# Eight transfers of the experts' weights in place of one, and no product of the mixture at place 2 of a chunk, in a two-layer GRU with a mixture of experts

## What is computed

```python
# part 1: two GRU layers over 1024 steps, batch 2, 256 features
mixed = tanh(x @ W_in.T + b_in + ctx)
h1 = gru(mixed, Wih0, Whh0, bih0, bhh0)    # r, z = sigmoid; n = tanh(xn + r * hn)
h2 = gru(h1, Wih1, Whh1, bih1, bhh1)       # h = (1 - z) * n + z * h, one step after the other
x = x + (gate[:, None, :] * h2 + h2) @ W_out.T + b_out
# part 2: one shared expert and 2 of 8 routed ones for each of the 2048 tokens
shared = silu(x @ w1) * (x @ w3) @ w2
s = sigmoid(concat(x, t_emb) @ router_W); top 2 of s + router_bias -> combine (N, 8)
routed = sum_e combine[:, e] * (gelu(x @ W1e[e]) @ W2e[e])
x = x + (shared + routed) / 3
```

## Time and profile before

| | us |
|---|---|
| median of 3 runs | 2195.91 (2191.42 to 2199.89) |
| the profiled execution | 2187.54 |
| its span | 2185.8 |
| TensorE busy in the span | 2068.4 |
| VectorE busy | 1841.5 |
| last state of layer 0 written (L424) | at 2116 |
| last state of layer 1 written | at 2156 |
| last group's work after that | to 2185.8 |
| instruction queue of TensorE (q8) | 548 packets, 8.98 MB |

### The profile page before, as it was taken

How to read it: one execution, slowest core, us unless ns; L and a number is a source line. 1 busy time by engine, 2 the same in 40 slices (tenths; PEclk the granted TensorE clock), 3 DMA queues, 4 the chain that set the end, 5 groups by cost and what they waited for, 6 DMA issues and landing times.

```text
span 2185.8 us, 162058 instructions
## 1 busy us (share of the span) xinstructions
PE 2068.4 (95%) x69920; PEld 1485.0 (68%) x69920; DVE 1841.5 (84%) x11225; ACT 1201.4 (55%) x6471; POOL 560.5 (26%) x2542
## 2 busy tenths in 40 slices
PE   6989899999999999999999999999999999999987
PEld 3666666677666776767767676666767676777766
DVE  4888889888888888888888888888888888888874
ACT  2555555555555555555555555555555555555542
POOL 1222232222322223222222222222232222222220
PEclk9999999999999999999999999999999999999999
DMA  5000000000000000000000000000000000000000
GB/s 219 4 4 5 4 5 5 24 5 5 9 5 24 5 5 10 5 24 5 10 5 24 5 5 9 5 24 5 5 10 5 24 5 10 5 21 9 5 16 19
DMA packets 10879, 32.76 MB, mean 15 GB/s; under 512 B 1368, under 2 KB 6832, under 8 KB 9136
## 3 DMA queue, kind: packets, MB, share of 16 engines
q1 hardware_dynamic: 10160, 22.38, 2.8%
HBM read 20.22 MB, written 2.16 MB: 10 GB/s over the span
## 4 chain that ended last, share of the span: by engine, by line
PE 60%; DVE 26%; ACT 10%; issue 3%; DMA 1%; SPq 0%; POOL 0%; DVEq 0%; POOLq 0%
PE bank L333 29%; PE bank L325 17%; PE bank L272 11%; DVE n_first L404 9%; DVE cells L424 7%; ACT factors L472 6%; ACT cells L476 4%; DVE r_pre L395 4%; DVE z_pre L405 3%; PE bank L306 3%; DVE bank L413 1%; DVE n_second L380 0%; DVE x L687 0%; PE bank L657 0%; DVE hid L745 0%
## 5 line engine op out<-in xcount | busy, mean ns | idle before, releaser
L333 PE MATMUL bank<-w_h,cells 128*22 128x128 f32 (+4 forms) x32768 | 1363.4, 281 | 23.6 <-DVE cells L424 13.9
L333 PEld LDWEIGHTS bank<-w_h,cells 128*22 128x22 f32 (+4 forms) x32768 | 853.0, 111 | 130.5 <-DVE cells L424 91.3
L325 PEld LDWEIGHTS bank<-w_h,cells 128*2 128x2 f32 (+15 forms) x28112 | 512.2, 113 | 528.1 <-DVE cells L424 502.8
L517 POOL TENSOR_SCALAR cells<-cells 128x4 f32<-128x4 f32 x2048 | 463.6, 226 | 1525.8 <-DVE cells L424 1524.8
L325 PE MATMUL bank<-w_h,cells 128*2 128x64 f32 (+15 forms) x28112 | 770.1, 225 | 76.3 <-DVE cells L424 55.5
L466 ACT ACTIVATE n_second<-r_pre 128x4 f32<-128x4 f32 x2048 | 426.3, 208 | 508.8 <-DVE r_pre L395 466.3
L472 ACT ACTIVATE factors<-z_pre 128x4 f32<-128x4 f32 x2048 | 429.6, 210 | 436.5 <-DVE z_pre L405 358.8
L404 DVE STREAM_TRANSPOSE n_first<-bank 128x64 f32<-128x64 f32 x2048 | 600.0, 293 | 33.1 <-PE bank L333 23.7
L424 DVE TENSOR_TENSOR_SCAN cells<-factors,cells 128x18 f32<-128x18 f32 x2048 | 397.2, 194 | 241.5 <-ACT cells L476 177.1
L395 DVE STREAM_TRANSPOSE r_pre<-bank 128x64 f32<-128x64 f32 x2048 | 480.6, 235 | 33.3 <-PE bank L325 24.9
L405 DVE STREAM_TRANSPOSE z_pre<-bank 128x64 f32<-128x64 f32 x2048 | 427.4, 209 | 0.0
(11 more groups left out here) (91 smaller groups left out, 558.8 us busy)
## 6 DMA issues: line engine op xcount, KB each, us to landing
c_all<-weights SPq DMA_DIRECT2D x6, 1024.0 KB
x_t<-in_x_t SPq DMA_DIRECT2D x4, 512.0 KB, 7.4
w_1e<-in_w_1e SPq DMA_DIRECT2D x1, 2048.0 KB
w_2e<-in_w_2e SPq DMA_DIRECT2D x1, 2048.0 KB
w_x<-in_w_x SPq DMA_DIRECT2D x2, 768.0 KB, 8.2
w_h<-in_w_h SPq DMA_DIRECT2D x2, 768.0 KB, 9.5
w<-in_w SPq DMA_DIRECT2D x3, 512.0 KB
out_y<-y SPq DMA_DIRECT2D x6, 256.0 KB, 3.5
```

What stands on the lines that cost most here:

```text
L325: mm = pe.matmul(r_sums[l][p][32 * g:32 * g + B * (j + 1)], state_tile(l, j, kt), w_h[l][:, kt, g, 2 * U:], start=False, stop=False, tile_ ...
L333: mm = pe.matmul(sums[l][p][32 * g:32 * g + B * (j + 1), 0:width], state_tile(l, j, kt), w_h[l][:, kt, g, 0:width], start=False, stop=Fals ...
L517: pool.tensor_scalar(cell_part(step_rows(l, j), 3), cell_part(step_rows(l, j), 1), 0.5, None, ALU.mult)\
```

## The change

The broadcast of a group's weights is cut into eight transfers, one for each expert, each issued when the one before has landed (by a wait of SP on a semaphore of their own, which is never cleared). Expert e's `hid` waits for its own transfer. The planner lets `hid` of expert 0 stand 8 half slots after `comb_t` and counts 2 more for each next expert, where it counted 12 for all; in the last group it counts 12 for all, as before. And in the groups of 128 steps (sparse windows) no product stands at place 2 of a chunk.

```diff
-    def transfer(self, name, after, took):
-        self.when[name], self.engine[name], self.value[name] = self.when[after] + took, "spread", 32
-        self.signals[name] = after
+    def transfer(self, name, after, took, value):
+        self.when[name], self.engine[name], self.value[name] = self.when[after] + took, "spread", value
...
         if engine == "pe":
-            return j in projection_pieces(part ^ 1) or part == 1 and (self.sparse or self.window > 5 * CH and j % 8 != 6)
+            return j in projection_pieces(part ^ 1) or self.sparse and j == 2 or part == 1 and (self.sparse or self.window > 5 * CH and j % 8 != 6)
...
-                    sp.dma_start(weights[:, 0:n], comb_t[0:E, 0:n]).then_inc(spread, 16)
-                if m == mix.when["comb_t"] // 2 + 1:
-                    sp.wait_ge(spread, 16)
-                    sp.dma_start(c_all[:, :, 0:n], weights[:, 0:n].partition_broadcast(P)).then_inc(spread, 16)
+                    sp.dma_start(weights[:, 0:n], comb_t[0:E, 0:n]).then_inc(s_spread, 16)
+                for e in range(E):
+                    if m == mix.when["comb_t"] // 2 + 1 + (e if mix is not mixtures[-1] else 0):
+                        sp.wait_ge(s_spread, mix.value[f"spread{e}"] - 16)
+                        sp.dma_start(c_all[:, e, 0:n], weights[e, 0:n].partition_broadcast(P)).then_inc(s_spread, 16)
...
-                            mix.add("dve", f"hid{u}_{m}{q}", (f"act{u}_{m if LAST else KT - 1}", f"down{u - 2}") + (("spread",) if i == m == q == 0 else ()),
+                            mix.add("dve", f"hid{u}_{m}{q}", (f"act{u}_{m if LAST else KT - 1}", f"down{u - 2}") + ((f"spread{i}",) if m == q == 0 else ()),
...
-            mix.transfer("spread", "comb_t", 12)
+            spread_before = 16 * (1 + E) * mixtures.index(mix)
+            for e in range(E):
+                mix.transfer(f"spread{e}", "comb_t", 8 + 2 * e if mix is not mixtures[-1] else 12, spread_before + 16 * (e + 2))
```

More of the change, by code:

```diff
@@ L70, in __init__ @@
         self.ops = {k: [] for k in ("pe", "act", "dve")}
-        self.when, self.value, self.engine, self.signals = {}, {}, {}, {}
-    def transfer(self, name, after, took):
-        self.when[name], self.engine[name], self.value[name] = self.when[after] + took, "spread", 32
-        self.signals[name] = after
+        self.when, self.value, self.engine = {}, {}, {}
+    def transfer(self, name, after, took, value):
+        self.when[name], self.engine[name], self.value[name] = self.when[after] + took, "spread", value
     def add(self, engine, name, waits, issue, beside=False, even=False):
@@ L100, in half @@
     def half(self, name):
-        return self.when[self.signals.get(name, name)] // self.window
+        return self.when[name] // self.window
     def total(self, engine, half):
@@ L108, in past_half @@
         mine = [o for o in self.ops[engine] if o[0] // self.window == half]
-        late = [k for k, o in enumerate(mine) if any(self.half(w) != half for w in o[2])]
+        late = [k for k, o in enumerate(mine) if any(self.half(w) != half for w in o[2] if self.engine[w] != "spread")]
         if late or half == 0:
@@ L218, in gru_moe_kernel @@
         s_hist = sem("s_hist")
+        s_spread = sem("s_spread")
         KINDS = ("r", "pe", "turn", "for_n", "n", "for_h", "h", "pool", "bias", "x", "xn", "go")
         sets = [[{k: sem(f"s_{k}{l}_{p}") for k in KINDS} for p in range(2)] for l in range(2)]
-        m_sets = [{k: sem(f"m_{k}_{p}") for k in ("pe", "dve", "act", "spread", "out", "go")} for p in range(2)]
+        m_sets = [{k: sem(f"m_{k}_{p}") for k in ("pe", "dve", "act", "out", "go")} for p in range(2)]
         def numbers(semaphores):
@@ L604, in sp_slots @@
                     sp.sem_inc(m_sets[half]["go"], 1)
-                spread = m_sets[mix.half("spread")]["spread"]
                 if m == mix.when["comb_t"] // 2:
                     wait_for(sp, mix, "comb_t")
-                    sp.dma_start(weights[:, 0:n], comb_t[0:E, 0:n]).then_inc(spread, 16)
-                if m == mix.when["comb_t"] // 2 + 1:
-                    sp.wait_ge(spread, 16)
-                    sp.dma_start(c_all[:, :, 0:n], weights[:, 0:n].partition_broadcast(P)).then_inc(spread, 16)
+                    sp.dma_start(weights[:, 0:n], comb_t[0:E, 0:n]).then_inc(s_spread, 16)
[3 more added lines that the diff above has]
+                        sp.dma_start(c_all[:, e, 0:n], weights[e, 0:n].partition_broadcast(P)).then_inc(s_spread, 16)
                 if m == mix.when[mix.y_done] // 2:
@@ L629, in wait_for @@
         def wait_for(eng, mix, name):
-            eng.wait_ge(m_sets[mix.half(name)][mix.engine[name]], mix.value[name])
+            if mix.engine[name] == "spread":
+                eng.wait_ge(s_spread, mix.value[name])
+            else:
+                eng.wait_ge(m_sets[mix.half(name)][mix.engine[name]], mix.value[name])
         def mixture_at(eng, engine, s, part, base):
```

## The result

The change makes the kernel slower by 0.4%: 2208.06 us against 2200.09, medians of 16 runs each on one chip, ratio 1.0037 (95% interval 1.0025 to 1.005). The forecast was 2185.0 with a range to 2194; it has the wrong sign. The profiled execution took 2205.99 us, its span is 2204.2.

What follows compares the result with a forecast made beforehand. The steps' scans set the pace (1.000 us each, 1.027 with mixture), with TensorE stalling for its own instructions behind broadcasts. Terms -12.0 + 0.8 - 2 - 0.3 + 2.6 = -10.9 us took 2195.91 to 2185.0; range 2176 to 2194.

Steps and rivals of the forecast that it cites:

- (f): Last group, which nothing hides: eight chained 64 KB pieces at 1.7 us each make the end 2.6 us later.
- rival 1: Last group's pieces cost 2.2 us each, so the tail grows by 6.6 us and the time is 2189.0; chance 0.17.
- (a): Steps: cutting the broadcast removes TensorE's stalls on its instruction blocks behind it, 12.0 us gained.
- (b): Steps: the pieces delay some of the 28 instruction blocks that pass by them, 0.8 us lost in all.
- rival 2: Steps: pieces hold instruction blocks up nearly as the whole did; from 0.43 us per block (a)'s gain is gone; chance 0.12.
- (c): Steps: SP's chained transfers come early enough that VectorE doesn't wait for weights; cost 0.
- (d): Groups with no product at place 2: instruction blocks end at other places, 2 us gained, bounds -5 and +4.
- (e): Group 7's plan ends 4 half slots earlier, so group 8 begins sooner; 0.3 us gained.
- Rival 3: Steps: the long stalls are a pause that comes anyway, not the broadcast's; time 2196.2; chance 0.06.

Runs made afterwards that it cites:

- e4: The changed kernel with each piece filling its 128 partitions from 128 different rows of x instead of one row of weights; 2182.76 us against 2186.32 before.
- e14: The kernel before with the eight rows of weights in DRAM 8 KB apart instead of 1 KB; ratio 1.037 to before.
- e10: e1 with eight copies of each weights row stored in DRAM, sixteen partitions of a piece reading each copy; ratio 1.0005 to the kernel before.
- e1: The changed kernel with the last group's weights in one broadcast again; ratio 0.9983 to the kernel before.
- e11: The kernel before with the broadcasts of groups 1 to 7 going to one partition instead of 128; ratio 0.9954 to before.
- a2: The changed kernel run once more without any edit; ratio 1.004 to the kernel before.
- e3: The changed kernel without the rule on place 2, so the eight transfers alone; ratio 1.0044 to the kernel before.
- e7: e1 without the rule for place 2; ratio 0.9974 to the kernel before.
- e12: e10 with the last group's store writing one copy and its one broadcast reading rows 1 KB apart again; ratio 0.996 to the kernel before.
- e13: e12 without the rule for place 2; ratio 0.9952 to the kernel before.
- e2: The kernel before with the rule on place 2 alone, the weights still in one broadcast; ratio 0.9994 to before.
- e8: The kernel before with 64 more matrix product calls at TensorE's start, which added 256 instructions; ratio 1.0035 to before.
- e5: The changed kernel with the last group's eight pieces issued without waiting for one another, the first `hid` waiting for all; 2186.89 us against 2186.32 before.

## Why the prediction was wrong, by its steps

**(f), the last group, failed, and decides the sign.** "One costs between the store's 1.21 (4 KB) and the output's 2.2 (128 KB); by bytes in between, 1.7." It cost 2.8, above the upper bound and above rival 1, and the term is +12.5 instead of +2.6. The bounds came from two transfers that read and write as many addresses as they have packets; a piece reads one row 128 times, which costs 12 ns a packet. e4 shows it by a piece of 1.8 us from different rows, e14 and e10 by a whole broadcast that took 14.09 and 14.31 us through its rows' distance, e1 by the end without the chain. The one broadcast hid this, since its eight rows were read beside each other. The Trainium skill, "DMA: Bandwidth & Descriptors", section "Anatomy of one DMA", gives a fit from which 64 KB are an estimated 2.15 us: nearer than my 1.7, still below the 2.8 measured, and above the 1.8 of e4. The section's fit is for transfers that GpSimd issues, which the prediction left out; these are SP's.

**(a), the broadcast's stalls, was right in mechanism and near in size.** -12.0; e11 gives -10.2 for those of groups 1 to 7 (10.4 less 0.2 of the end). The long waits went, as the change's waits show. Group 3 had one as well, which the prediction priced by its scans and did not list (2.19 us before 1204.8).

**(b), what the pieces cost in turn, was mis-sized.** +0.8; it is about +5. The five kernels with the change's pieces have steps of -6.7 (the change), -6.2 (a2), -3.8 (e1), -3.6 (e3) and -6.6 (e7) by the medians, against the -10.2 of (a) alone: +3.5 to +6.6. e12 and e13 have -9.5 and -10.3; they differ from e1 and e7 only in the copies, so the cost is in how the pieces read. The intervals of these pairs touch, so the cause is shown by all of them together and its size is rough. A piece I priced by its share of the bytes. But a group's broadcast was 128 packets of 8 KB with a train of 3.0 to 3.6 us in the groups of 128 steps, and the pieces are eight times 128 packets of 1 KB with trains of 1.5 us and more, so weights are under way for longer in all. They follow each other after 2.9 us instead of 1.9: group 0's take 23.5 us where the prediction had 15. That the blocks wait for them (e14) makes the cost is the likely way; no run shows it block by block. It is a mild form of rival 2: spread over the 28 blocks of the prediction it is 0.13 to 0.24 us for each, below the 0.43 that rival 2 wanted.

**(c), no wait of SP or VectorE in the steps, was right**: no wait for `c_all` stands there; VectorE waits for it in the last group alone.

**(d), the rule, -2:** e2 gives -2.2 with an interval that holds zero, e13 against e12 +1 the other way. Nothing that can be told from zero, and inside the bounds. The thought behind it, that the blocks' places are worth some us, no run tests, since e8 left them where they were.

**(e), group 7's earlier end, -0.3:** 12.68 instead of 13.05 us from the last scan to the store where the clock stays, so right, but 13.95 or 15.16 where it falls behind the pause. The term is -0.4 to +2.1, and I had not asked what a pause of 2.1 us does to the clock, though the earlier trace rows show it behind pauses of 2.3 to 2.7.

The sum by what was measured, with (b) in the middle of its span, (d) at nothing and (e) at a2's +0.9: -10.2 + 5 + 0.9 + 12.5 = +8.2; the medians say +8.0. The agreement is closer than the parts are known.

**Rival 3** falls with e11 and e14. The Trainium skill's "mostly hidden" ("Runtime: NRT & Kernel Launch", section "Instruction fetch mechanics") doesn't hold beside a transfer: up to 10.5 us of a block's crossing are open in e14's steps.

## What to carry to other kernels

Price a transfer by what it reads, not by bytes alone: if many packets read one row of DRAM, or rows 8 KB apart, take them one after another, and look for a trace's row of that same pattern before bounding it. Before a transfer is cut, look for the place where nothing hides it; there the pieces' fixed parts add up in full, and that place can be left whole while the others are cut (e1, e7, e13). On a kernel whose instructions stream in all the time, as this one's do, the time that a transfer is under way can cost at the next instruction block even when nobody waits for its data, so copies that let it finish sooner paid (e12, e13). And count what an edit really changes in the trace before reading it: e8 added twice the instructions it meant to, and e14 changed the packets of six groups together with the distance.

## What the runs showed of the hardware that I had not expected

- 128 reads of one DRAM row begin 12 ns apart, whatever their size (512 to 1024 bytes); 128 different rows begin within 0.5 us (e4, last group). In the last group rows 1 KB apart are read beside each other, rows 8 KB apart are not: 4.73 against 14.09 us for the same 1024 packets. The Trainium skill, "DMA: Bandwidth & Descriptors", section "Latency and other measured facts", tells of a like loss in copies with row pitches of 2 MiB and more and calls its cause an inference; here it shows at 8 KB, and the cause wasn't tried either.
- Eight rows of 1 KB without a gap between them were moved in packets of 8 KB, 128 for a broadcast; with gaps, in packets of a row each, 1024 (e14 and the earlier trace rows).
- An instruction block behind a transfer mostly came when 64% or more of its packets had begun, also with the 16 engines 44% busy: TensorE stood 7.8 to 10.5 us for it in e14.
- The same pause of 2.1 us was followed by full clock in some executions and half clock in others, 1.3 to 2.5 us apart.
- The same steps took 1703.2 to 1712.5 us in four executions, two of them on one chip (e5 and a2, 1703.6 and 1707.0); one trace doesn't price a change of 5 us there.
